# Issuing each token scatter of both expert routes only after the last but one has landed

## The reference

```
x = x + time_mix(layernorm(x))
x = x + ffn(layernorm(x), router_w, router_bias, wg, wu, wd, swg, swu, swd)
x = x + retention(layernorm(x))
x = x + ffn(layernorm(x), ... the same weights ...)

ffn: scores  = softmax(x @ router_w)                       # 64 experts
     idx     = top_k(x @ router_w + router_bias, 4)
     comb    = the 4 chosen scores, divided by their sum
     routed  = sum over chosen e: comb[e] * (silu(x @ wg[e]) * (x @ wu[e])) @ wd[e]
     shared  = the same form with two dense experts of 256 hidden units
     result  = routed + shared
```

## Time and profile before

| | |
|---|---|
| three runs | 1531.79 us median (1531.74 to 1532.27) |
| profiled execution, first to last instruction | span 1770.5 us |
| profiled execution's own time | none listed beside the span |
| mean granted TensorE clock | 0.866 |
| busy: PE / DVE / POOL / ACT | 1348.5 / 1091.4 / 921.4 / 687.1 us |
| route of moe1 / experts stage of moe1 | about 197 to 466 / 466 to 660 us |
| retention | about 660 to 1088 us |
| route of moe2 / experts stage of moe2 | about 1088 to 1335 / 1335 to 1700 us |

### The profile page before, as it was taken

The page is one execution under the profiler, slowest core; times in us unless marked ns, Lnnn a source line. Parts: engine busy times, 40 slices in busy tenths (PEclk is TensorE's granted clock), DMA queues, the critical chain, the costliest instruction groups (busy, mean ns, idle before and its releaser), DMA issues. The chain is left out here.

```text
span 1770.5 us, 24406 instructions
## 1 busy us (share of the span) xinstructions
PE 1348.5 (76%) x7408; PEld 924.2 (52%) x7408; DVE 1091.4 (62%) x2773; ACT 687.1 (39%) x1466; POOL 921.4 (52%) x1063
## 2 busy tenths in 40 slices
PE   6686656788699986998688985638876777777775
PEld 2344523455588873564456564325544555555533
DVE  5899755556366662473777775725654655555558
ACT  5998201111366652424133613111214444544420
POOL 3999364554555546656636032663453555555520
PEclk9898577889899998999799997869888888888878
DMA  9800531121788876112111003521136444443168
GB/s 363 343 1 0 201 136 56 71 86 61 207 276 265 271 250 185 57 46 69 39 53 39 3 1 128 219 101 49 68 97 185 148 140 140 140 134 105 40 238 272
DMA packets 109395, 233.81 MB, mean 132 GB/s; under 512 B 21543, under 2 KB 43470, under 8 KB 108756
## 3 DMA queue, kind: packets, MB, share of 16 engines
q1 hardware_dynamic: 81076, 164.03, 27.6%
q0 software_dynamic: 27648, 68.23, 11.3%
q10 hardware_dynamic: 544, 0.00, 0.0%
HBM read 125.44 MB, written 115.11 MB: 136 GB/s over the span
## 5 line engine op out<-in xcount | busy, mean ns | idle before, releaser
L882 POOL DMA_INDIRECT slots_x<-arena,slot x256 | 258.2, 1009 | 207.7 <-DVEq L981 131.4
L1248 POOL DMA_INDIRECT pairs_y<-arena x192 | 189.1, 985 | 177.2 <-DVE arena L1319 117.4
L1167 PE MATMUL moe_narrow<-arena 128*128 128x128 f32 x1536 | 232.7, 301 | 8.0 <-DVE arena L1311 6.7
L1311 DVE TENSOR_TENSOR arena<-arena,moe_narrow 64x128 f32<-64x128 f32 x384 | 111.6, 291 | 205.2 <-ACT arena L1215 186.3
L1167 PEld LDWEIGHTS moe_narrow<-arena 128*128 128x128 f32 x1536 | 212.9, 215 | 16.7 <-issue 15.0
L1156 PE MATMUL moe_narrow<-ident,arena 128*128 128x128 f32 x768 | 137.7, 308 | 92.8 <-ACT arena L1209 68.3
L707 PE MATMUL moe_wide<-arena 128*128 128x512 f32 x384 | 190.7, 644 | 22.0 <-DVE arena L1002 22.0
L1209 ACT ACTIVATE arena<-moe_narrow 128x512 f32<-128x512 f32 x192 | 114.6, 597 | 197.7 <-remote 117.8
L456 POOL DMA_INDIRECT arena<-slots_y,slot x128 | 128.7, 1005 | 87.0 <-DMA arena<-slots_y,slot 46.6
L1156 PEld LDWEIGHTS moe_narrow<-ident,arena 128*128 128x128 f32 x768 | 93.7, 155 | 146.8 <-issue 143.8
L799 ACT ACTIVATE arena<-moe_wide 128x512 f32<-128x512 f32 x48 | 28.7, 598 | 319.0 <-PE moe_wide L707 153.7
(11 more groups left out here) (318 smaller groups left out, 2410.4 us busy)
## 6 DMA issues: line engine op xcount, KB each, us to landing
arena<-slots_x SPq DMA_DIRECT2D x192, 264.0 KB, 3.8
slots_x<-arena SPq DMA_DIRECT2D x48, 528.0 KB, 15.8
slots_y<-arena SPq DMA_DIRECT2D x96, 256.0 KB, 3.7
arena<-w_gu SPq DMA_DIRECT2D x2, 8192.0 KB
arena<-pairs_y SPq DMA_DIRECT2D x32, 512.0 KB, 5.7
residual<-x SPq DMA_DIRECT2D x8, 512.0 KB
arena<-sw_gu SPq DMA_DIRECT2D x4, 1024.0 KB
slots_x<-arena,slot POOLq DMA_INDIRECT x256
```

Of the source, the lines that this page charges most:

```text
L882: pool.indirect_dma_start(out=x_slots, in_=xn[:, t, :], in_offset=None, out_offset=bass.IndirectOffsetOnAxis(ap=slot[:, t, i:i + 1], axis=0))\
L1167: last = pe.matmul(h_ps[n % 2][:, j * P:(j + 1) * P], weights[:, n % 3, j, h, :], xt[:, n % XTRING, (j * KH + h) * P:(j * KH + h + 1) * P] ...
L1248: pool.indirect_dma_start(out=slots.y_of, in_=ytile[:, n % YRING, j, :], in_offset=None, bounds_check=slots.pairs - 1, oob_is_err=False, o ...
```

## The change

The semaphores `landed0` to `landed7` give way to two, `landed_0` and `landed_1`, which the scatters count on in turn over the whole route. Ahead of each scatter from the third on, POOL waits until the one two before it has landed. The wait runs on over the blocks' borders. SP's waits for a block, and for the last one, ask for both semaphores. Both calls of `experts` take it. No transfer, no computation and no order of issue is changed.

```
@@ route_sync @@
                 if n < NB - 1:
-                    sp.wait_ge(sem(f"landed{n}"), LANDED)
+                    for parity in range(2):
+                        sp.wait_ge(sem(f"landed_{parity}"), LANDED // 2 * (n + 1))
                     if n < DONE:
                         sp.wait_ge(sem("tp_full"), KH * (n + 1))
@@ route_gpsimd @@
                     for i in range(K):
+                        if K * t + i >= 2:
+                            pool.wait_ge(sem(f"landed_{i % 2}"), 16 * ((K * t + i) // 2))
                         pool.indirect_dma_start(out=x_slots, in_=xn[:, t, :], in_offset=None,
                                                 out_offset=bass.IndirectOffsetOnAxis(ap=slot[:, t, i:i + 1], axis=0))\
-                            .then_inc(sem(f"landed{n}"), 16)
+                            .then_inc(sem(f"landed_{i % 2}"), 16)
@@ experts_sync @@
-            sp.wait_ge(sem(f"landed{NB - 1}"), LANDED)
+            for parity in range(2):
+                sp.wait_ge(sem(f"landed_{parity}"), LANDED // 2 * NB)
             load(0)
```

## The result

The change makes the kernel **slower: 1601.45 us** (median of 4 runs, 1598.73 to 1604.68) against 1532.03 for the kernel before beside it (4 runs, 1531.74 to 1536.08). The ratio is 1.0441, with a 95% interval of 1.0418 to 1.0463. The forecast was 1544 us, in a range of 1532 to 1554.

A forecast was written before the change was run, and what follows sets the result against it. POOL was taken to wait for DVE's slots in the routes, so that delay counts only in each route's last block. Terms 3 + 5 + 4 = +12 on 1531.8 gave 1544 us, range 1532 to 1554.

The forecast's parts named there:

- POOL becomes the route's bound: Rival, both routes: slots come early, moe2's POOL never catches up from block 0; +18 to +25, about 1554, chance 0.12.
- the prediction's own signs: Wrong in kind if ACT's remote waits shrink or the scatters' pitch reaches 1.48; in size if last-block landings aren't 4-6 us later.
- The wait with a free DMA: Scatters away from big loads: two take 2.65 us, 1.33 each, costing 1.0 us a block; upper bound 1.48 from the gathers.
- It wins back 2.9 a block: moe2's later blocks: period 24.2 against POOL's 21.3 lets a late POOL recover 2.9 us a block, 8.7 over three.
- Block 0 of moe2 beside w_gu: Last scatter starts at 1122.6 at the earliest, the power moves 11 to 15 us later; all hidden, cost 0.
- cover of 30.76 us: POOL's idling before the slots at 1216.85 in moe2, taken to hide the delay of the earlier blocks.
- The last block beside w_d: Each route's end: late landings beside the w_d loads stall POOL; +5 in moe2, +3 in moe1.
- upper bound (+10.6): Last block beside w_d: nothing lands until the loads are done, about 1331, so the last landing is 10.6 us later.
- 2.0 us of cover in moe1: moe1's end: SP loads 2.0 us after the last landing since it awaits the hand-over too, cutting +5 to +3.
- The same without the profiler: Routes: plain executions mostly lack ACT's unexplained waits, so POOL's cover is thinner and it ends late; +4.
- faster: Rival, ACT's L799 in each block: two under way shorten ACT's unknown waits; about 1529, or near 1470; chance 0.12.
- 254 scatters: The prediction's count of scatters that get a wait ahead of them.

The follow-up runs named there:

- r5: The changed kernel unchanged, run where the kernel before is at the upper level: 1709.43 us, ratio 0.9684 against the kernel before.
- r15: The kernel before, unchanged, traced again at the lower level: 1530.08 us, span 1528.4.
- r6: The changed kernel with block 0 of each route free of the wait, upper level: 1693.63 us, ratio 0.9613 against the kernel before.
- r12: The changed kernel with block 0 of each route free of the wait, lower level: 1580.44 us, ratio 1.0321 against the kernel before.
- r1: The kernel before, unchanged, profiled again at the upper level: 1770.85 us, span 1769.2, beside a median of 1759.95.
- r9: The kernel before with a small POOL memset finished ahead of each scatter, no landing waits, upper level: 1717.01 us, ratio 0.978.
- r10: The kernel before with two semaphores in turn in each block and no wait added on POOL, upper level: 1758.98 us, ratio 0.9981.
- r16: The kernel before with a small POOL memset finished ahead of each scatter, no landing waits, lower level: 1539.39 us, ratio 1.0049.

## Why the prediction was wrong, point by point

The sign was right, forecast with a chance of 0.75. The mechanism that won was the rival "POOL becomes the route's bound" (0.12), and I had sized it at 18 to 25 where 69 were measured. By the prediction's own signs it is wrong in kind: the pitch of the scatters passes the gathers' 1.48, and at the upper level the remote waits shrink (r5). Of the 69.4 us, block 0 has 31.2 (forecast 0), blocks 1 to 6 have 21.2 (forecast 4) and the ends 17.0 (forecast 8).

- **The wait with a free DMA** (2.65 for two, 1.33 each): right for a quiet pair (2.69), wrong as a mean. Blocks 1 to 6 of moe2 take 147.8 us for 96 scatters, 1.54 each, above the upper bound of 1.48. The step that failed took one landing, 2.4, as the time of all. Landings of 3 to 6 us also occur, at DMA shares of 0.21 (1109 to 1115) and 0.23 (1145 to 1151), and each is now felt. I set a block at 21.3 us; it takes 24.6 (147.8 / 6). Some of the late ones stand beside SP's 256 KB load of w_d at each block's border: it starts at 1105.0, 1130.0, 1154.4 and 1179.5, and the landings from 1105.52, 1130.68, 1155.03 and 1180.03 take 3.28, 2.98, 4.23 and 3.33. Others, such as 4.04 from 1110.33 and 4.32 from 1145.98, have no such load beside them; what makes these late is not settled. The figure of the Trainium skill ("DMA: Bandwidth & Descriptors", "Anatomy of one DMA") gives an estimate of 2.3 us for such a transfer, which agrees with the quiet 2.42 and says nothing of the late ones. By it this term would have been zero.
- **"It wins back 2.9 a block"**: this step failed, and the next one with it. It set a compute period of 24.2 against 21.3 for POOL. The period was right: the slots of moe2 come every 23.8 us in r15. POOL's 21.3 was wrong, and the 20.2 (16 x 1.26) that it grew from is no block at this level: without waits POOL takes 22.5, with them 24.6. So paced POOL doesn't win back 2.9 a block, it falls behind the slots by 24.6 - 23.8 = 0.8; before it won back 1.3. The difference of the two kernels is 2.1 a block, 12.6 over six, and nothing of block 0's delay was ever recovered.
- **Block 0 of moe2 beside w_gu, "hidden, 0"**: failed, and it is the largest miss. The last scatter was to start at 1122.6 at the earliest, 30.7 us after the first; it starts 42.6 after (1076.03 against 1033.46), since two under way get their landings at 11.35, 8.86 and 7.90 us each. And it isn't hidden: +23.0 in moe2, +8.2 in moe1. The power starts 44.1 us after the block's first scatter (1077.55), 23 later than before and not 11 to 15. The cover of 30.76 us belongs to the kernel before at the upper level; even there the changed kernel's POOL waits for slots 7.5 us in all (r5), and block 0 free gives back 16 us (r6). At the level of the result r12 shows the price of the waits in it, 21 us.
- **The last block beside w_d** (+5 in moe2, +3 in moe1): right in mechanism, undersized: 8.8 and 8.2. The last of the chain's rows above has the stall, 8.48 us for one landing; the upper bound (+10.6) held. The 2.0 us of cover in moe1 were of the upper level: in r15 SP loads at 404.02, 3.8 us after the last scatter's start.
- **"The same without the profiler"** (+4): the thought that plain executions have none of the remote waits was right, but for the wrong reason: it is the chip's level and not the profiler (r1, r15). I used it for one term, where the whole cover of the route should have been counted again without these waits: 220.1 - 160.1 = 60 us less for moe2's seven blocks.
- **The rival "faster"**: its mechanism exists. At the upper level the waits of ACT shrink and the change gains 3.2% (r5). It was ruled down because the scatters "come as densely as before (1.33 against 1.26)"; but a lower rate of the scatters is part of what spares ACT (r9 against r10), and the real pitch is 1.5. What the Trainium skill ("Runtime: NRT & Kernel Launch", "Instruction fetch mechanics") says of instruction blocks isn't borne out or refuted by any run; their queue has the same 62 packets in after. One of these lies in each of the late stretches from 1110.33 and from 1145.98, and none in the quiet one from 1120.55; whether it delays a landing was not tested.
- **The rule of the Trainium skill** ("DMA: Bandwidth & Descriptors", "Rules for kernel authors": issue early, wait late) speaks against the change, and at the level of the result the runs agree: no limit, four and two under way give 1534, 1559 and 1601. At the upper level they don't: 1760, 1776 and 1709.
- **"254 scatters"**: the wait stands ahead of 126 in each route, 252 in all. Nothing hangs on it.

What was foretold of the profile after: gaps alternating 0.30 and 0.47 (forecast 0.4), gaps of several us beside w_gu, SP's first load 31.3 us after the last block's first scatter (forecast 28). POOL's wait for the slots didn't shrink to 20, it vanished in moe2.

## What to carry to other kernels

A wait for landings turns every late transfer into a stall of the issuing engine, so price it with the mean and the tail of the landings, and beside each big load with that load's own stretch, never with the quiet landing alone. Before calling a delay hidden, compare the engine's period with that of what feeds it at the level of the times: when the span of a trace is far from the median of the runs, its idle time is not cover. If an issuer is to be spaced, a fixed spacing that keeps its block below its feeder's period is far cheaper (r16, 22.4 us against 23.8, +6 us) than a wait for its own landings (24.6, +69 with the stalls at the loads).

## What was not expected of the hardware

- The same kernel takes 1532 us on some chips or sessions and 1760 on others (the lower level in the result and two more sessions, the upper in the first trace and three more; within a session the runs stay within 1.2% of their median, but for one run of 6805 us). In the slow ones ACT and DVE have waits whose release the profile doesn't place: 34.80 us in the earlier trace rows, where the product that ACT's instruction needs had ended 30 us before, 135.1 us in twelve waits in r1, none in r15. Not everything is slower there: up to the first route the levels agree (first scatter at 219.2 us in r1 and 220.0 in r15, granted clock 0.91 and 0.90 over the first 190 us). Over the whole span the clock is lower on the slow level (0.877 against 0.924). The waits in the routes shrink when the scatters are spaced or paced (r9, r5). That PE's semaphore updates are what comes late was argued and not tested, and what puts a chip on that level is open.
- Scatters of 132 KB each beside an 8 MB load take 11.35, 8.86 and 7.90 us to land in place of 2.43, and beside the last loads of w_d 8.48, though at most two are under way. With sixteen queued, the same block of 16 was issued in 19.5 us and block 1 could start 24.9 us after block 0.
